# Attention units batch by batch, with the first batch's head work in the FFN up phase

## What is computed

```
x = x + xattn(layernorm(x), ctx, ctx)      # an mLSTM attention, 16 heads of 32
x = x + ffn(layernorm(x))                  # FP4 weights, 512 -> 2 x 1408 -> 512
```

```
C = (q k^T / sqrt(32)) * D
Cn = C / (max(|sum C|, exp(-max_log_D)) + 1e-6)
h = Cn v;   hn = (h - mean) * rsqrt(var + 1e-6) * ln_scale     # over the 32 of a head
```

## Time and profile before

| | |
|---|---|
| median of 3 runs | 647.42 us (647.1 to 650.89) |
| the profiled execution | 646.62 us, of it 644.6 us span from first to last instruction |
| granted TensorE clock | 0.891 of full, mean |
| TensorE (PE) | 546.7 us busy, 85% |
| VectorE | 453.5 us, 70% |
| GpSimd | 317.2 us, 49% |
| ScalarE | 298.9 us, 46% |
| DMA | 39.96 MB, mean 62 GB/s |
| chain that ended last | PE 49%, DVE 28%, issue 8%, ACT 5%, POOL 4% |

### The profile page before, as it was taken

One profiled execution on the slowest core, in us unless ns is written; L12 is line 12 of the kernel. 1 busy time (PEld: TensorE's weight loads), 2 busy tenths in 40 slices (PEclk: granted clock), 3 DMA queues, 4 the chain that ended last, 5 costly groups with the idle time before them and its releaser, 6 DMA issues.

```text
span 644.6 us, 7996 instructions
## 1 busy us (share of the span) xinstructions
PE 546.7 (85%) x2638; PEld 316.9 (49%) x2638; DVE 453.5 (70%) x741; ACT 298.9 (46%) x646; POOL 317.2 (49%) x341
## 2 busy tenths in 40 slices
PE   3628999827999995998999995979999969877997
PEld 3227889414666543444666444336666434322342
DVE  4877774994888798545888896536888873688601
ACT  3164435425777701355776513346777201655300
POOL 2213332542677665204776861235776840488700
PEclk9855558866999998898999996998999998999999
DMA  8044120106410300036102100064100001200000
GB/s 216 12 123 156 51 66 14 54 0 198 164 33 2 132 1 1 33 124 237 66 2 89 42 1 1 33 216 166 46 2 2 1 0 50 82 1 0 1 33 33
DMA packets 20883, 39.96 MB, mean 62 GB/s; under 512 B 7275, under 2 KB 7915, under 8 KB 20331
## 3 DMA queue, kind: packets, MB, share of 16 engines
q1 hardware_dynamic: 20842, 39.46, 18.2%
HBM read 30.93 MB, written 4.33 MB: 55 GB/s over the span
## 4 chain that ended last, share of the span: by engine, by line
PE 49%; DVE 28%; issue 8%; ACT 5%; POOL 4%; DMA 2%; SPq 2%; DVEq 0%; POOLq 0%; ACTq 0%
PE pf L893 14%; PE po L835 9%; PE pf L905 8%; PE pq L803 7%; POOL ffn L497 3%; DVE tok L1144 3%; DVE bst L1003 2%; DVE ffn L1182 2%; PE pq L765 2%; PE pq L815 2%; DVE ffn L1178 2%; ACT th L637 2%; DVE hT L1222 2%; PE pq L840 2%; DVE tok L1158 2%
## 5 line engine op out<-in xcount | busy, mean ns | idle before, releaser
L905 PE MATMUL pf<-w_down,hT 128*128 128x512 f32 x352 | 154.3, 596 | 0.0
L497 POOL TENSOR_TENSOR ffn<-ffn,ts 128x512 f32<-128x512 f32 x88 | 111.8, 1271 | 69.9 <-DVE ffn L1182 62.5
L893 PE MATMUL pf<-yT,gu_val 128*128 128x512 f16 x544 | 136.8, 390 | 10.9 <-DVE ffn L1178 7.6
L630 ACT ACTIVATE ts<-pf,gu_scale 128x512 f32<-128x512 f32 x136 | 86.4, 686 | 59.6 <-PE pf L893 59.2
L905 PEld LDWEIGHTS pf<-w_down,hT 128*128 128x128 f32 x352 | 66.5, 191 | 83.6 <-issue 78.0
L459 POOL TENSOR_SCALAR_AFFINE_SELECT dmat<-dmat 128x512 f32<-128x512 f32 x64 | 43.3, 679 | 89.9 <-ACT dmat L596 89.8
L893 PEld LDWEIGHTS pf<-yT,gu_val 128*128 128x128 f16 x544 | 48.7, 99 | 78.1 <-DVE ffn L1182 15.5
L596 ACT ACTIVATE dmat<-negm,aT 128x128 f32<-128x128 f32 x256 | 80.2, 395 | 8.2 <-DMA negm<-negm_dram 8.2
L835 PEld LDWEIGHTS po<-v_sb,dmat 128*128 128x128 f32 x512 | 70.5, 215 | 5.3 <-issue 1.7
L835 PE MATMUL po<-v_sb,dmat 128*128 128x33 f32 x512 | 69.4, 294 | 0.0
L502 POOL TENSOR_TENSOR hT<-ffn,th 128x512 f32<-128x512 f32 x44 | 64.5, 1468 | 0.0
(11 more groups left out here) (120 smaller groups left out, 744.2 us busy)
## 6 DMA issues: line engine op xcount, KB each, us to landing
negm<-negm_dram SPq DMA_DIRECT2D x32, 512.0 KB, 5.2
ffn<-in_x SPq DMA_DIRECT2D x4, 1024.0 KB, 6.5
ctx_sb<-in_ctx SPq DMA_DIRECT2D x4, 1024.0 KB, 5.4
x_sb<-in_x SPq DMA_DIRECT2D x4, 1024.0 KB, 5.4
x_res<-x_sb SPq DMA_DIRECT2D x4, 1024.0 KB, 4.8
out<-x_res SPq DMA_DIRECT2D x16, 256.0 KB, 2.0
x_res<-in_L_ffn_gate_up_packed SPq DMA_DIRECT2D x1, 704.0 KB, 6.0
th<-in_L_ffn_down_packed SPq DMA_DIRECT2D x1, 352.0 KB, 6.6
```

Source lines behind the costliest of these rows:

```text
L497: pool.tensor_tensor(acc, acc, ts[:, h % TDEEP, 1], ALU.add).then_inc(tsum_ready, 1)
L630: act.activation(ts[:, h % TDEEP, g], bank(q, h, g), ACT.Copy, scale=gu_scale[:, g * GU + o:g * GU + o + 1]).then_inc(t_ready, 1)
L893: last = pe.matmul(bank(q, h, g), gu_val[:, h // 2 + h % 2 * FT, g], yT[:, part, g], start=(part == 0), stop=(part == 1))
L905: last = pe.matmul(pf[:, tt], hT[:, j, tt * P:(tt + 1) * P], w_down[:, j], start=(j == 0), stop=(j == FT - 1))
```

## The change

- The units go batch by batch: the head group is u % 4 and the batch u // 4, so batch 0 of a pair is complete with unit 3, in step 9.
- The work behind the values (`post`, `norm2_sums`, `norm2`) is split by batch. That of batch 0 is cut into steps 0 to 5 and spread over steps 10 to 20 of the up phase (`HALF_STEPS`); that of batch 1 stays in the tail (`second_half`). On GpSimd the products with `ln_scale`, the residual and the power of batch 0 move to steps 12, 16 and 18.
- `add_later` moves from VectorE to GpSimd, ahead of the mask of the same step.
- In `post`, the squared norm and its product with EPS become one instruction, and the division by 32 is folded into the next one.
- `osq` gets a buffer of its own, for one batch, with a semaphore `osq_read`; ScalarE's first square moves to step 11. For its space `TDEEP` goes from 4 to 3.
- TensorE no longer has five matmuls of down tile 2 ahead of the next pair's turns; all 11 stand behind `gate_sums`.

The line `hg, b = u // 2, u % 2` becomes `hg, b = u % KT, u // KT` in all eight places (SP, GpSimd, ScalarE, TensorE, VectorE). The rest of the diff, cut:

```diff
-TDEEP = 4
+TDEEP = 3
...
-SQUARES = {SCORES_AT[-2] + 3: 0, SCORES_AT[-1] + 3: 1}
+HALF_AT = SCORES_AT[KT - 1] + 3
+HALF_STEPS = {HALF_AT: 0, HALF_AT + 2: 1, HALF_AT + 3: 2, HALF_AT + 4: 2, HALF_AT + 5: 2, HALF_AT + 6: 3,
+              HALF_AT + 8: 4, HALF_AT + 10: 5}
+SQUARES = {HALF_AT + 1: 0, SCORES_AT[-1] + 3: 1}
 SPARE = 19
...
-BEFORE_TURNS, BEFORE_BACK = 5, 5
+BEFORE_BACK = 5
...
-            def post(p):
-                if isinstance(p, int) and p == 0:
+            def add_later(p, u):
+                hg, b = u % KT, u // KT
+                pool.wait_ge(o_read, UNITS * p + u + 1)
+                pool.wait_ge(later_ready, UNITS * p + u + 1)
+                o = tok[:, 2 * b + 1, hg * HG:(hg + 1) * HG, :]
+                pool.tensor_tensor(o, o, later[:, u % 2], ALU.add).then_inc(o_whole, 1)
+
+            def by_ln_scale(p, b):
+                if isinstance(p, int) and p == 0 and b == 0:
                     pool.wait_ge(s_const, 16 * 7)
-                for tt in range(TT):
-                    pool.wait_ge(osq_ready, 2 * p + 1 + tt // 2)
+                pool.wait_ge(osq_ready, 2 * p + 1 + b)
+                for tt in (2 * b, 2 * b + 1):
                     o = tok[:, tt, :, 0:DH]
                     pool.tensor_tensor(o, o, ln_row[:].rearrange("q (h d) -> q h d", d=DH), ALU.mult
                                        ).then_inc(ols_ready, 1)
 
+            def residual1(p, b):
+
                 pool.wait_ge(s_x, 16 * p + 16)
-                for tt in range(TT):
+                for tt in (2 * b, 2 * b + 1):
                     pool.wait_ge(oscaled, TT * p + tt + 1)
                     xt = x_sb[:, tt].rearrange("q (h d) -> q h d", d=DH)
                     pool.tensor_tensor(xt, xt, tok[:, tt, :, 0:DH], ALU.add).then_inc(x1_ready, 1)
 
-            def norm2(p):
-                pool.wait_ge(var2_ready, p + 1)
-                pool.tensor_tensor(rs[:, 1], vv[:, 1], neghalf[:, 0:TT], ALU.pow).then_inc(rstd2_ready, 1)
+            def norm2(p, b):
+                c = slice(2 * b, 2 * b + 2)
+                pool.wait_ge(var2_ready, 2 * p + b + 1)
+                pool.tensor_tensor(rs[:, 1, c], vv[:, 1, c], neghalf[:, c], ALU.pow).then_inc(rstd2_ready, 1)
...
-                    if p is not None and h in MASKS:
-                        mask(p, MASKS[h])
+                    if p is not None:
+                        if h in ADD:
+                            add_later(p, ADD[h])
+                        if h in MASKS:
+                            mask(p, MASKS[h])
+                        step = HALF_STEPS.get(h)
+                        if step == 1:
+                            by_ln_scale(p, 0)
+                        if step == 3:
+                            residual1(p, 0)
+                        if step == 4:
+                            norm2(p, 0)
                     if q is None and h == 14:
                         rstd1(n)
                 if q is None:
-                    post(p)
-                    norm2(p)
+                    by_ln_scale(p, 1)
+                    residual1(p, 1)
+                    norm2(p, 1)
                     centre_v(n)
                     return
                 if q is not None:
                     gated(q, FT - 1)
                 if p is not None:
-                    post(p)
+                    by_ln_scale(p, 1)
+                    residual1(p, 1)
                 if n is not None:
                     rstd1(n)
                 if p is not None:
-                    norm2(p)
+                    norm2(p, 1)
                 if q is not None:
...
-                hg, b = u // 2, u % 2
+                hg, b = u % KT, u // KT
                 if half == 0:
                     act.wait_ge(s_negm[u % 4], 32 * p + 16 * (u // 4) + 16)
                     act.wait_ge(aT_ready, p + 1)
-                    if u >= 2:
+                    if UNITS * p + u >= 2:
                         act.wait_ge(pv_done, UNITS * p + u - 1)
-                    elif not (isinstance(p, int) and p == 0):
-                        act.wait_ge(hvar_ready, p)
...
             def squares(p, b):
 
-                act.wait_ge(o_whole, UNITS * p + UNITS - 1 + b)
-                act.wait_ge(pv_done, UNITS * p + UNITS - 1 + b)
+                act.wait_ge(o_whole, UNITS * p + KT * (b + 1))
+                if 2 * p + b:
+                    act.wait_ge(osq_read, 2 * p + b)
                 g = slice(b * 2 * NH, (b + 1) * 2 * NH)
-                act.activation(osq[:, g], tok[:].rearrange("q t h d -> q (t h) d")[:, g, 0:DH], ACT.Square
+                act.activation(osq[:], tok[:].rearrange("q t h d -> q (t h) d")[:, g, 0:DH], ACT.Square
                                ).then_inc(osq_ready, 1)
...
                 if q is not None:
                     down(q, 0, range(FT))
                     down(q, 1, range(FT))
-                    down(q, 2, range(BEFORE_TURNS))
                 if n is not None:
                     turn_x(n, 0)
                 if p is not None and q is not None:
@@ -972,7 +994,7 @@
                     turn_x(n, 1)
                     gate_sums(n)
                 if q is not None:
-                    down(q, 2, range(BEFORE_TURNS, FT))
+                    down(q, 2, range(FT))
                     down(q, 3, range(BEFORE_BACK))
...
             def later_part(p, u):
-                hg, b = u // 2, u % 2
+                hg, b = u % KT, u // KT
                 dve.wait_ge(pv_done, UNITS * p + u + 1)
                 if u == 0:
                     dve.wait_ge(floor_ready, 2 * p + 2)
+                if UNITS * p + u >= 2:
+                    dve.wait_ge(o_whole, UNITS * p + u - 1)
...
-            def add_later(p, u):
-                hg, b = u // 2, u % 2
-                dve.wait_ge(o_read, UNITS * p + u + 1)
-                dve.wait_ge(later_ready, UNITS * p + u + 1)
-                o = tok[:, 2 * b + 1, hg * HG:(hg + 1) * HG, :]
-                dve.tensor_tensor(o, o, later[:, u % 2], ALU.add).then_inc(o_whole, 1)
-
-            def post(p):
+            def head_norms(p, b):
                 link = po_steps.link
-                po_steps.start(p)
-                sums = tok[:].rearrange("q t h d -> q (t h) d")
-                dve.wait_ge(o_whole, UNITS * p + UNITS)
-
-                link(dve.scalar_tensor_tensor(hn[:, 0], sums[:, :, DH], -1.0, sums[:, :, DH],
-                                              ALU.mult, ALU.max))
-                link(dve.tensor_tensor(hn[:, 1], hn[:, 0], floor[:].rearrange("q b c h -> q (b c h)"),
+                if b == 0:
+                    po_steps.start(p)
+                g = slice(b * 2 * NH, (b + 1) * 2 * NH)
+                sums = tok[:].rearrange("q t h d -> q (t h) d")[:, g, DH]
+                dve.wait_ge(o_whole, UNITS * p + KT * (b + 1))
+
+                link(dve.scalar_tensor_tensor(hn[:, 0, g], sums, -1.0, sums, ALU.mult, ALU.max))
+                link(dve.tensor_tensor(hn[:, 1, g], hn[:, 0, g], floor[:, b].rearrange("q c h -> q (c h)"),
                                        ALU.max))
-                link(dve.tensor_scalar(hn[:, 1], hn[:, 1], EPS, None, ALU.add))
-                link(dve.tensor_tensor(hn[:, 2], hn[:, 1], hn[:, 1], ALU.mult))
-                dve.wait_ge(osq_ready, 2 * p + 2)
-                link(dve.tensor_reduce(hn[:, 0], osq, AX.X, ALU.add))
-                link(dve.tensor_scalar(hn[:, 1], hn[:, 0], 1.0 / DH, None, ALU.mult))
-
-                dve.scalar_tensor_tensor(hn[:, 3], hn[:, 2], EPS, hn[:, 1], ALU.mult, ALU.add
+                link(dve.tensor_scalar(hn[:, 1, g], hn[:, 1, g], EPS, None, ALU.add))
+                link(dve.scalar_tensor_tensor(hn[:, 2, g], hn[:, 1, g], EPS, hn[:, 1, g], ALU.mult, ALU.mult))
+
+            def head_var(p, b):
+                link = po_steps.link
+                g = slice(b * 2 * NH, (b + 1) * 2 * NH)
+                dve.wait_ge(osq_ready, 2 * p + b + 1)
+                dve.tensor_reduce(hn[:, 0, g], osq[:], AX.X, ALU.add).then_inc(osq_read, 1)
+                dve.wait_ge(osq_read, 2 * p + b + 1)
+
+                dve.scalar_tensor_tensor(hn[:, 3, g], hn[:, 0, g], 1.0 / DH, hn[:, 2, g], ALU.mult, ALU.add
                                          ).then_inc(hvar_ready, 1)
-                dve.wait_ge(hvar_ready, p + 1)
-
-                link(dve.tensor_scalar(hn[:, 3], hn[:, 3], VAR_MAX, None, ALU.min))
-                link(dve.tensor_scalar(hn[:, 0].bitcast(I32), hn[:, 3].bitcast(I32), 1, None,
+                dve.wait_ge(hvar_ready, 2 * p + b + 1)
+
+                link(dve.tensor_scalar(hn[:, 3, g], hn[:, 3, g], VAR_MAX, None, ALU.min))
+                link(dve.tensor_scalar(hn[:, 0, g].bitcast(I32), hn[:, 3, g].bitcast(I32), 1, None,
                                        ALU.logical_shift_right))
-                link(dve.tensor_scalar(hr[:].bitcast(I32), hn[:, 0].bitcast(I32), -1.0, RSQRT_START,
+                link(dve.tensor_scalar(hr[:, g].bitcast(I32), hn[:, 0, g].bitcast(I32), -1.0, RSQRT_START,
```

(52 more changed lines are left out.)

35 lines of the change are left out of this document (24 added, 11 removed).

## The result

The changed kernel took **674.53 us** (median of 4 runs, 669.43 to 675.51) against 647.71 us for the kernel before on the same chip: 1.0393 times as long, 95% interval 1.0345 to 1.0441. The profiled execution took 674.13 us, span 672.4. Forecast were 671 us, 649 to 686, and slower at 0.75.

What follows compares the result with a forecast made beforehand. TensorE bounds the up phase with VectorE almost full, and VectorE is one chain from step 0 to `yn`; 2 x 8.7 + 9.5 - 2.4 = +24.5 us on 646.62 gives 671 us, range 649 to 686.

Steps and rivals of the forecast that it cites:

- U: Shift of the last `gate`, the end of VectorE's up phase, in iteration 2: forecast 12.3 us later.
- the tail gave 7.6 against 7.2: VectorE's work behind the up phase: moving batch 0's part out was to save 7.2 us.
- R2: Rival: the up phase absorbs the whole first half, as TensorE's queue tolerates later `products`; 634 us, chance 0.13.
- R1: Rival: the 17 tiny instructions slip into GpSimd's pauses at their price alone, 4.4 us together; 651 us, chance 0.18.
- R3: Rival: every tiny instruction meets GpSimd, 1.15 us each; 697 us, chance 0.09.
- VectorE without waits from step 10 on: Sign in the changed profile: VectorE's idle time from step 10 is filled, with TensorE waiting for it in steps 11 to 21.
- The price of a small operation: Steps 10 to 20: 17 tiny VectorE instructions at 0.65 us each, 11.0 us; sign, `newton`'s three at 0.5 to 0.8.
- three quarters of the 0.53: Stretch beside GpSimd added to a tiny instruction's 0.26 us alone; 0.53 is what the same stretch's adds pay.
- the rule of the Trainium skill: Two-port tensor_scalar or two-SBUF-input VectorE instructions wait for GpSimd's whole running instruction; without it U 1.2 lower, 667 us.
- Edits priced at nothing: Add on GpSimd, unit order, `TDEEP` 3, earlier squares, semaphores: no cost; add uncovered would be 3.4 us an iteration.
- TensorE's order: Five down matmuls moved behind the gate sums: +3.6 us in iterations 1 and 2, +4.4 in iteration 3.
- "-2.4 us": Iteration 0 gains: 4.5 us of steps 0, 1 and two `newton` vanish in waits, GpSimd handovers add some 2.1.

Runs made afterwards that it cites:

- e_newton_doubled: Changed kernel with `newton` done twice in each of steps 13, 14 and 15 for the first batch: 680.4 us, ratio 1.05.
- h_unlocked_sums_first: Kernel before with VectorE's tail reordered, the next pair's statistics and the reduce ahead of the first four small operations: 643.69 us, ratio 0.9935.
- l_after_squares_at_20: Changed kernel with ScalarE's squares of the second batch at step 20 in place of step 18: 672.99 us, ratio 1.0358.
- f_ln_scale_one_column: Changed kernel with GpSimd's product by ln_scale for the first batch cut to one column of each head: 663.97 us, ratio 1.0233.
- b_turns_behind: Kernel before with only all 11 matmuls of down tile 2 moved behind the gate sums: 657.63 us, ratio 1.0149.
- d_order_add_tdeep: Kernel before with batch-first units, the later-part add on GpSimd and TDEEP 3: 657.29 us, ratio 1.0125.
- k_add_squares_at_20: d_order_add_tdeep with ScalarE's squares of the second batch at step 20 instead of 18: 649.91 us, ratio 1.0029 against the kernel before.

## Why the prediction came out as it did

**The chain.** Right: VectorE's chain sets the end of the up phase from step 10 on, and what is put into it is paid in full. U came to 11.5 and 11.6 us against 12.3, the tail gave 7.6 against 7.2, the first four small operations of the tail kept 4.87 us (389.92 to 394.79) against 4.85. R2 is refuted by the windows, R1 (4.4) and R3 (19.6) by the 9.39 us. "Paid in full" holds for the instructions, but the sum closes partly by luck, as two of its terms are off in opposite directions. The small operations cost 1.6 us less than priced. And 3.6 us of VectorE's waits were to be filled; from its first instruction of step 10 to the last `gate` it waits 4.5, 4.2 and 4.2 us before and 3.4, 1.9 and 2.9 after (iterations 1 to 3, waits over 0.15 us), so 1.1, 2.3 and 1.3 were filled. The sign "VectorE without waits from step 10 on" did not come.

**The price of a small operation.** 0.65 against 0.55 measured: right in size, wrong in form. It is not a price for each but one for each GpSimd operation met, as `e_newton_doubled` shows; of `newton`'s three, none took the 0.5 to 0.8 us named as the sign in step 14, but 0.18, 1.14 and 0.19. The held operation ends with GpSimd's, and the prediction had that sentence; three quarters of the 0.53 was a guess where the number of GpSimd's operations in each step could have been counted in the trace before. The cap and the shift took 1.09 and 1.10 us beside GpSimd, so the trace agrees with the rule of the Trainium skill, page "SBUF — State Buffer", section "Who interferes with whom", which the prediction had weighed. The same section says that a reduce never contends on this chip: the half reduce took 1.21 us beside L509, and on that `h_unlocked_sums_first` is built.

**Edits priced at nothing.** Order and buffers were. The add was not, in itself: priced was GpSimd's time and VectorE's wait, not ScalarE's, whose squares of step 18 wait for the last add with the copies of step 19 queued behind. In the changed kernel VectorE's longer chain covers most of this; 0.50 and 0.58 us of its waiting are left, 1.3 us an iteration by `l_after_squares_at_20`. So U was right with this step missing from it, which is luck.

**TensorE's order.** Forecast 3.6, 3.6 and 4.4, measured 4.0, 3.6 and 2.7 behind `yn`. In iteration 3 the turn follows a wait of only 1.57 us and keeps its clock. That an open wait for `yn` would cost clock was in none of my terms: in iterations 1 and 2 the turns stand at half clock behind it, and undoing the order gave 4.2 and 4.3 us there. The wait itself was 2.52 us, where I had written near 4.

**Iteration 0, the step that failed:** "-2.4 us". It became +2.0, all of it ahead of `yn`. I had put steps 0 and 1 into VectorE's waits of up to 3.49 us; but step 1 stands ahead of the `products` of unit 6, and in this iteration TensorE waits for these, 2.27 us. The wait is shown; how much of the 4.4 us it is can't be said, since the clock moves this mark by 10 us between kernels. With the wait taken away the forecast's gain did not come either, so the cause stays open.

**Iteration 3.** U is 14.1, where iteration 2 has 11.5. Of these 2.6 us, 2.0 are there by the end of step 4, ahead of all moved work (iteration 3 is 1.4 us later than before at that mark, iteration 2 0.6 earlier): half clock stands at the start of its up phase for longer. The other 0.6 lie behind; TensorE is at half clock again at 505 to 514 us (0.51 in the window 505 to 515).

## What to carry to other kernels

Before moving small operations of VectorE, count the GpSimd operations that run under them, and put what isn't held (reduces, statistics) there instead; that order alone made this kernel 0.65% faster. When an operation changes engine, follow its result to every waiter, and look at what is queued behind the waiter on a third engine. Work that fills TensorE's wait can also keep its clock: in the changed kernel, taking it away cost its own length, and the clock behind the wait; in the kernel before, which waited 7.11 us anyway, its own length alone.

## What I had not expected of the hardware

TensorE's clock can fall within a full phase after a short wait: 1.74 us at 353.72 to 355.46, then half clock from 357.00 on, 2.86 us for 16 records and 3.62 for 8. After 1.06 us in the same place (`f_ln_scale_one_column`) it stayed whole. But the length of the one wait does not decide it: in the same iteration of the changed kernel waits of 1.66, 1.59 and 1.74 us (ending at 374.12, 380.62 and 392.40) were each followed by full clock. In the first 110 us the full clock comes back at another moment from kernel to kernel, also where the code up to there is the same (before and `b_turns_behind`: next up phase at 151.6 and 148.9) or differs in the place of one operation (`d_order_add_tdeep` and `k_add_squares_at_20`: 153.0 and 159.1). The same happens early in the up phases: at the end of step 4, with nearly the same work up to there, the kernels stand apart by up to 4.9 us (iteration 1: -0.2 to +4.7 against before; iteration 3: -1.8 to +2.9). A change of less than 1% needs several runs, and a profile cut at marks.
